# The last norm of a two-layer graph network: one-hot rows moved from ScalarE to VectorE, one row load of four moved from SyncE to ScalarE, Newton's steps once per seven batches

## The chip, the cores and the metric

The kernel runs on one core of one Trainium2 chip. The metric is the device time of one execution in microseconds, lower is better; a run's time is the median of several executions. The engines are named TensorE (PE in the profile; PEld is its weight load), VectorE (DVE), ScalarE (ACT), GpSimd (POOL) and SyncE (SP). A "q" behind a name (SPq, ACTq) is the instruction queue of that engine, from which DMAs are issued.

## The reference, cut to what matters

There are 100,000 nodes with 32 features and 25,000 edges. Two layers run one after the other, and each ends in a residual sum and a layer norm without learned weights:

```python
def _layernorm(x, axis=-1, eps=1e-05):
    m = jnp.mean(x, axis=axis, keepdims=True)
    v = jnp.var(x, axis=axis, keepdims=True)
    return (x - m) / jnp.sqrt(v + eps)
...
    x = _layernorm(x + _L0_gnn_ref(x, edge_weight1, edge_index, ...))
    x = _layernorm(x + _L1_gnn_ref(x, edge_weight, edge_attr_3, edge_index, ...))
```

The second layer makes a message per edge and adds it to the row of the edge's destination node (`out.at[dst].add(msg)`). The change is in what follows the messages: the adding into the nodes' rows, the second norm and the store of the result.

## The kernel before, in words

A window is 512 nodes, kept as 128 partitions of 4 nodes with 32 features, so 128 x 128 numbers; there are 196 windows (`NW`), all of them resident in on-chip memory in the tile `res`. A batch is G = 4 windows, so 128 x 512 numbers, and there are NB = 49 batches. The edges were sorted by destination window into 196 tiles of 128 rows in the DRAM tensor `placed[1]`, each row with 128 payload numbers and 8 more (`ROW` = 136 numbers, 544 bytes), the first of which says where the row belongs. Messages already have their mean taken away, so that the last norm needs only the sum of squares.

The last stage works through the 49 batches in a pipeline over five engines. Each engine has its instructions in an order written out by hand: `staged(stages, n)` (line 70) runs, in step s, the stages from the last to the first, stage k for batch s - k. Engines meet only through semaphores. For a batch b, before the change:

- SyncE (lines 498 to 500, helper `first_rows` at 374) waits until batch b - 6 has been multiplied, reads four tile numbers from memory into registers (line 376), and issues four loads (line 380), one for each window, into `pw4[b % 6]`, a ring of six. Each load is 68 KB.
- GpSimd (`apart_4`, 593) waits for the four loads and takes the difference between the window's first row and the place numbers: a 128 x 4 tile `kr4`, a ring of three. Before it, in the same step, stands `scale_4` (587) of ten batches earlier, which multiplies 128 x 512 numbers of `res` by 1/sqrt into `out4`, a ring of three.
- ScalarE (`away_from_4`, 804) takes |column - place| in four instructions of 128 columns into `away4`, then (`hot_4`, 811) max(0, 1 - that) in one of 512 columns: one-hot rows in `oh4`. Five steps after the first it squares the batch (`square_4`, 794), and eleven steps after it issues the store of the batch (`store_4`, 799), 256 KB.
- TensorE (1048 to 1053) multiplies the four one-hot tiles by the four payload tiles into a bank of PSUM.
- VectorE adds the bank to `res` (`add_4`, 1440) and three steps later sums the squares over 32 features (`norm_4`, 1445). Behind every fourth batch it runs `newton` (1338 to 1351): one addition, one shift-like step and three rounds of three instructions, eleven in all, each waiting for the one before, on 128 x 64 numbers (16 for each batch). The remainder, batch 48, gets eleven instructions of its own.

The waits that close the rings and that the prediction speaks of: a load waits for the multiplication five batches back (`z_mm`), `scale_4` waits for `z_root` of its group and for the store that left its buffer of `out4` (`z_st`).

## Time and profile before

| what | us |
|---|---|
| median of three runs (lowest, highest) | 1985.52 (1982.97, 1986.45) |
| span of the profiled execution, first to last instruction | 1707.1 |
| what lies around it, by the median less the span | 278.4 |
| the last stage in that span, from the first row load to the last instruction | about 151 |

The profile gives the profiled execution no total beside its span, so its own time is read as the span and the 278.4 us around it. In the page, busy time is the time in which an engine had an instruction in execution; instructions that read registers, wait for semaphores or issue DMAs are not counted, and are found in the timeline and in the chain of work under SPq, ACTq and DVEq. Durations overlap a little: the next instruction of an engine can start some 0.09 us before the end that is recorded for the one before.

### The profile page before, as it was taken

The page shows a single profiled execution, that of the slowest core. Times are in us where ns is not written, and L with a number is a line of the kernel's source. Part 1 is how long each engine was busy: PE and PEld are TensorE (multiplying, and loading weights), DVE is VectorE, ACT ScalarE, POOL GpSimd, SP SyncE. Part 2 cuts the span into 40 slices and gives each one's busy share as a digit, 9 for nine tenths or more (in the row PEclk, how much of TensorE's full clock was granted, in tenths as well). Part 3 has the DMA queues.
Part 4 walks back from the last instruction along what each step waited for, and adds up shares of the span by engine and source line. Part 5 has one row for each costly group of instructions (what it writes and reads, how often), then busy time and mean ns, then how long its engine had stood idle before and what let it go on. Part 6 is the DMA issues. An engine that isn't in the chain of part 4 may idle for free.

```text
span 1707.1 us, 25367 instructions
## 1 busy us (share of the span) xinstructions
PE 1315.9 (77%) x6200; PEld 957.6 (56%) x6200; DVE 1193.5 (70%) x3648; ACT 858.9 (50%) x2256; POOL 1068.9 (63%) x1168
## 2 busy tenths in 40 slices
PE   5699993686513777665778999958999999996673
PEld 1388881242212555554655666635777777775563
DVE  9699995677512443676667999964777777774776
ACT  0167770011101222666775777735666666664884
POOL 7777778777777777774111444448877887830444
PEclk8599996577555999888888999977999999997655
DMA  1000000123224988665555666531222222213785
GB/s 41 13 14 13 14 14 20 47 72 79 67 68 127 257 250 246 171 174 145 132 138 140 179 184 189 163 95 32 58 58 57 58 64 67 59 42 78 196 216 157
DMA packets 298498, 178.98 MB, mean 105 GB/s; under 512 B 28715, under 2 KB 290032, under 8 KB 298352
## 3 DMA queue, kind: packets, MB, share of 16 engines
q1 hardware_dynamic: 219712, 116.54, 26.0%
q0 software_dynamic: 29008, 36.18, 8.3%
q10 hardware_dynamic: 49632, 24.65, 5.0%
q8 instruction: 51, 0.84, 0.2%
q14 instruction: 95, 0.78, 0.2%
HBM read 111.18 MB, written 66.07 MB: 104 GB/s over the span
## 4 chain that ended last, share of the span: by engine, by line
PE 42%; POOL 28%; issue 16%; DVE 8%; DMA 2%; DVEq 2%; SPq 1%; ACT 1%; POOLq 0%; ACTq 0%
PE bank L1025 12%; POOL gat L511 12%; POOL lined L518 11%; PE bank L994 7%; PE bank L1018 7%; DVE res L1308 5%; PE bank L945 3%; POOL out L591 3%; PE bank L947 3%; PE bank L1034 3%; PE bank L1003 3%; PE bank L987 3%; DMA placed<-pay,pos_i 1%; DVEq L1308 1%; DVEq L1302 1%
## 5 line engine op out<-in xcount | busy, mean ns | idle before, releaser
L566 POOL DMA_INDIRECT gat<-x_d,src_i x196 | 253.2, 1292 | 59.0 <-issue 53.1
L511 POOL DMA_INDIRECT gat<-in_x,key_i x196 | 211.1, 1077 | 64.8 <-issue 62.4
L1308 DVE TENSOR_TENSOR res<-res,bank 128x128 f32 x588 | 168.4, 286 | 108.5 <-issue 24.4
L528 POOL DMA_INDIRECT placed<-pay,pos_i x196 | 191.9, 979 | 68.1 <-issue 65.6
L518 POOL DMA_INDIRECT lined<-in_x,other_i x196 | 195.8, 999 | 59.7 <-issue 59.7
L1025 PE MATMUL bank<-prod,ident 128*128 128x280 f32 x896 | 217.0, 400 | 0.0
L1025 PEld LDWEIGHTS bank<-prod,ident 128*128 128x128 f32 x896 | 171.0, 191 | 46.5 <-issue 0.6
L956 PE MATMUL bank<-woh,pw 128*128 128x128 f32 x784 | 135.4, 335 | 69.3 <-DVE woh L1287 33.4
L956 PEld LDWEIGHTS bank<-woh,pw 128*128 128x128 f32 x784 | 120.3, 238 | 85.5 <-DVE woh L1287 44.5
L56 ACT ACTIVATE xt<-bank 128x128 f32<-128x128 f32 x98 | 26.6, 271 | 269.6 <-PE bank L897 261.2
L1018 PE MATMUL bank<-rw,ht 65*128 65x384 f32 x392 | 141.3, 514 | 23.3 <-ACT ht L738 13.8
L553 POOL TENSOR_TENSOR hx<-hid,xin 128x512 f32<-128x512 f32 x49 | 62.0, 1264 | 136.2 <-ACT hid L724 136.2
L878 PE MATMUL bank<-tile_oh,sel 128*128 128x196 f32 x784 | 143.0, 337 | 3.1 <-ACT tile_oh L651 2.0
L878 PEld LDWEIGHTS bank<-tile_oh,sel 128*128 128x128 f32 x784 | 131.0, 193 | 17.3 <-issue 17.0
L1130 DVE SCALAR_TENSOR_TENSOR junk<-iota,w_f,bank 128x196 f32<-128x196 f32 x392 | 138.0, 408 | 0.9 <-PE bank L869 0.9
L994 PE MATMUL bank<-hid,wsl 128*128 128x512 f32 x294 | 134.9, 594 | 0.4 <-ACT hid L724 0.4
L56 ACT ACTIVATE rsb<-bank 128x384 f32<-128x384 f32 x196 | 95.5, 491 | 52.7 <-PE bank L1018 45.6
L1052 PE MATMUL bank<-pw,oh 128*128 128x128 f32 x392 | 89.6, 400 | 41.3 <-ACT oh L814 39.9
L689 ACT ACTIVATE woh<-iota,kr 128x128 f32<-128x128 f32 x294 | 93.8, 390 | 52.6 <-PE bank L956 26.0
L1018 PEld LDWEIGHTS bank<-rw,ht 65*128 65x128 f32 x392 | 75.8, 200 | 75.0 <-issue 17.9
L724 ACT ACTIVATE hid<-bank,bias 128x512 f32<-128x512 f32 x147 | 101.1, 688 | 31.2 <-PE bank L994 31.2
L1138 DVE TENSOR_TENSOR pay<-bank,wjs 128x512 f32<-128x512 f32 x49 | 33.8, 689 | 115.1 <-PE bank L902 115.0
(204 smaller groups left out, 2840.5 us busy)
## 6 DMA issues: line engine op xcount, KB each, us to landing
pw<-placed SPq DMA_DIRECT2D x588, 68.0 KB, 2.1
pw<-placed SPq DMA_DIRECT2D x98, 272.0 KB
xin<-in_x_t SPq DMA_DIRECT2D x53, 256.0 KB, 3.2
placed<-pay SPq DMA_DIRECT2D x49, 272.0 KB, 2.4
x_d<-res POOLq DMA_DIRECT2D x49, 256.0 KB, 3.8
placed<-pay SPq DMA_DIRECT2D x28, 448.0 KB, 3.2
out<-out ACTq DMA_DIRECT2D x49, 256.0 KB, 2.7
xin<-in_x_t ACTq DMA_DIRECT2D x45, 256.0 KB, 3.6
```

The lines of the kernel that those rows point to most:

```text
L56: return act.activation(out, in_, ACT.Copy)
L511: pool.indirect_dma_start(gat[:, t, :], None, x, bass.IndirectOffsetOnAxis(ap=key_i[:, 0, t:t + 1], axis=0)).then_inc(s_gat, 16)
L518: pool.indirect_dma_start(lined[i % LINED][:, k, :], None, x, bass.IndirectOffsetOnAxis(ap=other_i[:, t:t + 1], axis=0)).then_inc(s_lined[ ...
L528: pool.indirect_dma_start(placed[1].rearrange("t p r -> (t p) r"), bass.IndirectOffsetOnAxis(ap=pos_i[:, 1, t:t + 1], axis=0), pay[i % 4][ ...
L566: pool.indirect_dma_start(gat1[g % 3][:, k, :], None, x1_d, bass.IndirectOffsetOnAxis(ap=src_i[:, t:t + 1], axis=0)).then_inc(c_gat[g % 3] ...
L878: ins = pe.matmul(psum[4 + 2 * v][:, 0:NT], sel[g % 2][:, k, v, :], tile_oh[g % 2][:, k, :], start=t == 0, stop=t == NT - 1)
L956: ins = pe.matmul(quarter(bank, k), pw[i % 6][:, k, 0:P], woh[i % 4][:, k, :], start=True, stop=True)
L994: pe.matmul(psum[BANK[n][h]][:, :], wsl[:, 2 + n, :], hid[n - 1][h][:, :], start=True, stop=True).then_inc(m_mm[n], 1)
L1018: pe.matmul(psum[n % 3][:, 0:RC], ht[g % 2][:, P * k:P * k + P], rw[:, :, :].rearrange("p a b -> p (a b)"), start=True, stop=True).then_in ...
L1025: ins = pe.matmul(psum[3 + g % 2][:, 0:40 * U].rearrange("p (t u) -> p t u", t=U), ident[:, :], prod[g % 2][:, :, v, :], start=v == 0, sto ...
L1130: dve.scalar_tensor_tensor(out=junk[n % 4][:, :], in0=iota[:, :], scalar=w_f[:, c, t:t + 1], in1=column(n), op0=ALU.is_equal, op1=ALU.mult ...
L1308: add.up(dve.tensor_tensor(into, into, quarter(bank + k // G, k % G), ALU.add))
```

## The change: what it does, and the diff

One-hot rows. ScalarE's five instructions of a batch go, with the tile `away4` and the semaphore `z_away`. In their place VectorE compares, in one instruction of 512 columns, the column number with `kr4` (now place less window), both in on-chip memory. It stands last in VectorE's step, behind the square sum of four batches earlier and the addition of two batches earlier.

Row loads. SyncE reads three tile numbers and issues three loads; ScalarE reads the fourth number and issues the fourth load. It stands last in ScalarE's step, behind the store of 14 batches earlier and the square of 5 batches earlier. A new semaphore `z_stored` holds ScalarE's first load until SyncE has seen the stores of the stage before.

Newton's steps. They run once for seven batches, on 128 x 112 numbers, so seven times and not thirteen. `scale_4` moves from ten to thirteen batches behind `apart_4`.

```diff
+BY_SP = 3
+TOGETHER = 7
...
-        def first_rows(sp, to, c, b, landed):
+        def first_rows(eng, on, to, c, b, ks, landed):
             _, tiles = nc.values_load_multi_w_load_instructions(
-                t0_i[0:1, c, G * b:G * b + G], engines=[mybir.EngineType.SP], min_val=0, max_val=NT,
+                t0_i[0:1, c, G * b + ks.start:G * b + ks.stop], engines=[on], min_val=0, max_val=NT,
                 skip_runtime_bounds_check_because=IN_RANGE)
-            for k in range(G):
-                sp.dma_start(to[:, k, :], placed[c][bass.ds(tiles[k], 1)].rearrange("t p r -> p (t r)")).then_inc(landed, 16)
+            for k, tile in zip(ks, tiles):
+                eng.dma_start(to[:, k, :], placed[c][bass.ds(tile, 1)].rearrange("t p r -> p (t r)")).then_inc(landed, 16)
...
             sp.wait_ge(c_mm, NU)
+            sp.sem_inc(z_stored, 1)
             for b in range(NB):
                 wait(sp, z_mm, b - 5)
-                first_rows(sp, pw4[b % 6], 1, b, z_pw[b % 6])
+                first_rows(sp, mybir.EngineType.SP, pw4[b % 6], 1, b, range(BY_SP), z_pw[b % 6])
...
             def scale_4(b):
-                pool.wait_ge(z_root, b // 4 + 1)
+                pool.wait_ge(z_root, b // TOGETHER + 1)
...
             def apart_4(b):
                 pool.wait_ge(z_pw[b % 6], 16 * G * (b // 6 + 1))
-                wait(pool, z_away, b - 2)
-                pool.tensor_tensor(kr4[b % 3][:, :], w128[:, G * b:G * b + G], pw4[b % 6][:, :, P], ALU.subtract).then_inc(z_kr, 1)
-            staged([apart_4] + [None] * 9 + [scale_4], NB)
+                wait(pool, z_oh, b - 2)
+                pool.tensor_tensor(kr4[b % 3][:, :], pw4[b % 6][:, :, P], w128[:, G * b:G * b + G], ALU.subtract).then_inc(z_kr, 1)
+            staged([apart_4] + [None] * 12 + [scale_4], NB)
...
-            def away_from_4(b):
-                act.wait_ge(z_kr, b + 1)
-                wait(act, z_oh, b - 1)
-                for k in range(G):
-                    ins = act.activation(away4[b % 2][:, k, :], iota[:, 0:P], ACT.Abs, bias=kr4[b % 3][:, k:k + 1])
-                ins.then_inc(z_away, 1)
-            def hot_4(b):
-                act.wait_ge(z_away, b + 1)
-                wait(act, z_mm, b - 2)
-                act.activation(oh4[b % 3][:, :, :], away4[b % 2][:, :, :], ACT.Relu, bias=1.0, scale=-1.0).then_inc(z_oh, 1)
-            staged([away_from_4, hot_4, None, None, None, square_4] + [None] * 5 + [store_4], NB)
+            act.wait_ge(z_stored, 1)
+            def load_4(b):
+                wait(act, z_mm, b - 5)
+                first_rows(act, mybir.EngineType.Activation, pw4[b % 6], 1, b, range(BY_SP, G), z_pw[b % 6])
+            staged([load_4] + [None] * 4 + [square_4] + [None] * 8 + [store_4], NB)
...
             def norm_4(b):
-                four, o = b // 4, G * J * (b % 4)
+                n, o = b // TOGETHER, G * J * (b % TOGETHER)
                 dve.wait_ge(z_sq, b + 1)
...
-                if b % 4 == 3 or b == NB - 1:
+                if b % TOGETHER == TOGETHER - 1:
                     dve.wait_ge(z_ssq, b + 1)
-                    wait(dve, z_out, 4 * (four - 1))
-                    newton(vps4[:, 0:n], root4[four % 2][:, 0:n], newt4[:, 0:n], ssq4[four % 2][:, 0:n], z_root)
-            staged([add_4, None, None, norm_4], NB)
+                    wait(dve, z_out, TOGETHER * (n - 1))
+                    newton(vps4[:, :], root4[n % 2][:, :], newt4[:, :], ssq4[n % 2][:, :], z_root)
+            def hot_4(b):
+                dve.wait_ge(z_kr, b + 1)
+                wait(dve, z_mm, b - 2)
+                dve.tensor_tensor(oh4[b % 3][:, :, :], iota[:, 0:P].unsqueeze(1).broadcast_to([P, G, P]),
+                                  kr4[b % 3][:, :].unsqueeze(2).broadcast_to([P, G, P]), ALU.is_equal).then_inc(z_oh, 1)
+            staged([hot_4, None, add_4, None, norm_4], NB)
```

## Rows read from the trace of the kernel before

**Rows 1.** Span; windows: us, PE, PEld, DVE, ACT, POOL busy, PEclk, DMA, GB/s

```profile
span 1707.1 us, 25367 instructions
...
1553.00:1708.00 155.00, 92.34 (x405) 79.33 (x404) 100.59 (x248) 112.31 (x294) 59.51 (x98) 0.62 0.66 172
...
1620.00:1640.00 20.00, 14.69 (x64) 12.72 (x63) 15.80 (x38) 19.33 (x52) 10.09 (x17) 0.60 0.86 225
```

**Rows 2.** Waits in the last stage, in total, times, longest

```profile
POOL kr L596 <- DMA pw<-placed: 98.8, 42, 34.2
...
SPq L376 <- PE bank L1052: 1.1, 3, 0.6
```

**Rows 3.** Chain of work, SyncE's row loads: start us, us, what

```profile
1558.93 0.33 SPq L380
1559.45 0.33 SPq L380
...
1561.32 0.33 SPq L380
```

**Rows 4.** Timeline, GpSimd, first and last place difference: start us, us, what

```profile
1560.05 0.20 POOL L596 TENSOR_TENSOR kr<-w,pw 128x4 f32<-128x4 f32 x1 [34.20 <-DMA pw<-placed]
...
1681.94 0.20 POOL L596 TENSOR_TENSOR kr<-w,pw 128x4 f32<-128x4 f32 x1 [2.00 <-DMA pw<-placed]
```

**Rows 5.** Groups by line, last stage: busy us, mean ns, idle before

```profile
L808 ACT ACTIVATE away<-iota,kr 128x128 f32<-128x128 f32 x196 | 62.4, 389 | 28.5 <-POOL kr L596 27.9
L591 POOL TENSOR_TENSOR out<-res,root 128x512 f32<-128x512 f32 x49 | 51.2, 1049 | 15.1 <-DVE root L1348 11.3 <-ACT away L808 2.6 <-DMA out<-out 1.0
...
L814 ACT ACTIVATE oh<-away 128x512 f32<-128x512 f32 x49 | 30.1, 614 | 0.1
L797 ACT ACTIVATE sq<-res 128x512 f32<-128x512 f32 x49 | 30.1, 614 | 2.7 <-DVE ssq L1448 2.7
```

**Rows 6.** Timeline, one batch on GpSimd and VectorE

```profile
1626.35 0.20 POOL L596 TENSOR_TENSOR kr<-w,pw 128x4 f32<-128x4 f32 x1
1626.37 0.68 DVE L1443 TENSOR_TENSOR res<-res,bank 128x512 f32<-128x512 f32 x1
1626.50 1.05 POOL L591 TENSOR_TENSOR out<-res,root 128x512 f32<-128x512 f32 x1
...
1626.97 0.68 DVE L1448 TENSOR_REDUCE ssq<-sq 128x16 f32<-128x512 f32 x1
```

**Rows 7.** Timeline, VectorE around one run of Newton's steps, and its narrow form

```profile
1580.55 0.69 DVE L1448 TENSOR_REDUCE ssq<-sq 128x16 f32<-128x512 f32 x1 [2.49 <-ACT sq L797]
...
1583.80 0.23 DVE L1348 SCALAR_TENSOR_TENSOR root<-newt,root 128x64 f32<-128x64 f32 x1
1583.94 0.68 DVE L1443 TENSOR_TENSOR res<-res,bank 128x512 f32<-128x512 f32 x1
...
1698.02 0.17 DVE L1348 SCALAR_TENSOR_TENSOR root<-newt,root 128x16 f32<-128x16 f32 x1
```

**Rows 8.** Timeline, VectorE and GpSimd starting together

```profile
1633.36 0.29 POOL L596 TENSOR_TENSOR kr<-w,pw 128x4 f32<-128x4 f32 x1 [1.09 <-DMA pw<-placed]
1633.36 0.23 DVE L1344 TENSOR_TENSOR newt<-root 128x64 f32<-128x64 f32 x1
...
1682.10 1.05 POOL L591 TENSOR_TENSOR out<-res,root 128x512 f32<-128x512 f32 x1
1682.25 0.97 DVE L1344 TENSOR_TENSOR newt<-root 128x64 f32<-128x64 f32 x1
```

**Rows 9.** Chain of work: a register load on VectorE behind a compute instruction

```profile
1547.58 1.09 DVE pay L1420
1548.67 0.54 DVEq L1302
```

**Rows 10.** DMA issues, last stage: count, KB each, median us to landing

```profile
pw<-placed SPq DMA_DIRECT2D x196, 68.0 KB, 2.1
```

**Rows 11.** Timeline, one batch's multiplication at the lower clock

```profile
1583.29 2.08 PE L1052 MATMUL bank<-pw,oh 128*128 128x128 f32 x8 [1.05 <-ACT oh L814]
```

More of the change, by code:

```diff
@@ L38 @@
 IN_RANGE = "a prefix sum of counts that add up to the number of rows"
-assert NT == NW and NG * G == NT and NB == NG and 2 * HT == NT and NG % 7 == 0
+assert NT == NW and NG * G == NT and NB == NG and 2 * HT == NT and NG % 7 == 0 and NB % TOGETHER == 0
 assert PAD_NODE + NT * P - E <= NPAD <= OTHER and NPAD * P < 1 << 24
@@ L253, in gnn_kernel @@
         out4 = ring(sb, "out4", 3, [P, BC])
-        ssq4 = ring(sb, "ssq4", 2, [P, 4 * G * J])
-        root4 = ring(sb, "root4", 2, [P, 4 * G * J])
-        vps4 = sb("vps4", [P, 4 * G * J])
-        newt4 = sb("newt4", [P, 4 * G * J])
+        ssq4 = ring(sb, "ssq4", 2, [P, TOGETHER * G * J])
+        root4 = ring(sb, "root4", 2, [P, TOGETHER * G * J])
+        vps4 = sb("vps4", [P, TOGETHER * G * J])
+        newt4 = sb("newt4", [P, TOGETHER * G * J])
         psum = [ctx.enter_context(nc.psum_tensor(f"bank{n}", [P, 512], F32)) for n in range(8)]
@@ L291, in gnn_kernel @@
         c_prod, c_sum, c_scal, c_pay, c_mm, c_msg = sem("c_prod"), sem("c_sum"), sem("c_scal"), sem("c_pay"), sem("c_mm"), sem("c_msg")
[L293 removed]
+        z_pw, z_kr, z_oh, z_mm, z_stored = ring(sem, "z_pw", 6), sem("z_kr"), sem("z_oh"), sem("z_mm"), sem("z_stored")
         z_y, z_sq, z_ssq, z_root, z_out = sem("z_y"), sem("z_sq"), sem("z_ssq"), sem("z_root"), sem("z_out")
@@ L446, in _ @@
                 freed(sp, b - 5)
-                first_rows(sp, pw[b % 6], 0, b, s_pw[b % 6])
+                first_rows(sp, mybir.EngineType.SP, pw[b % 6], 0, b, range(G), s_pw[b % 6])
             def load_extra(i, c):
@@ L463, in _ @@
                 wait(sp, s_back, min(i - 5 - D_EXTRA, NG))
-                first_rows(sp, pw[i % 6], 1, b, s_pw[i % 6])
+                first_rows(sp, mybir.EngineType.SP, pw[i % 6], 1, b, range(G), s_pw[i % 6])
                 if b >= 5:
@@ L1445, in norm_4 @@
             def norm_4(b):
-                four, o = b // 4, G * J * (b % 4)
+                n, o = b // TOGETHER, G * J * (b % TOGETHER)
                 dve.wait_ge(z_sq, b + 1)
-                dve.tensor_reduce(ssq4[four % 2][:, o:o + G * J], nodes(sq4[b % 3][:, :]), AX_X, ALU.add).then_inc(z_ssq, 1)
-                if b % 4 == 3 or b == NB - 1:
-                    n = o + G * J
+                dve.tensor_reduce(ssq4[n % 2][:, o:o + G * J], nodes(sq4[b % 3][:, :]), AX_X, ALU.add).then_inc(z_ssq, 1)
+                if b % TOGETHER == TOGETHER - 1:
                     dve.wait_ge(z_ssq, b + 1)
-                    wait(dve, z_out, 4 * (four - 1))
-                    newton(vps4[:, 0:n], root4[four % 2][:, 0:n], newt4[:, 0:n], ssq4[four % 2][:, 0:n], z_root)
-            staged([add_4, None, None, norm_4], NB)
+                    wait(dve, z_out, TOGETHER * (n - 1))
[6 more added lines that the diff above has]
+            staged([hot_4, None, add_4, None, norm_4], NB)
 _INS = ["x", "src", "dst", "edge_attr_3", "edge_weight", "edge_weight1",
```

4 lines of the change are left out of this document (1 added, 3 removed).

## The prediction

> **What bounds the kernel now.** The change touches only the last stage, so I read the windows first. The stage takes the last 155 us of a span of 1707.1 us, and no engine fills it: ScalarE is busy 112 us, VectorE 101, GpSimd 60 [rows 1]. No engine being full, I looked for a queue. In the waits, GpSimd's place difference waits 98.8 us for row loads, 34.2 of it the one wait ahead of the stage, while SyncE waits for TensorE 1.1 us in all [rows 2]: the loads are late, and not because a buffer is missing. The chain of work shows why. SyncE issues a load every 0.52 us and starts the next batch's 2.39 us after the last batch's [rows 3]. That is its register read and four issues, one behind the other. The place differences are 121.9 us apart from first to last, 2.54 us a batch [rows 4], against 48 x 2.39 = 114.7 from issue alone; I put the other 7 us down to hiccups. So SyncE's issue sets the pace. Just under it lies ScalarE, busy 19.33 us of 20 in the middle of the stage [rows 1].
>
> **The base of the sum.** The profiled execution is its span, 1707.1, and what lies around it, which I take as 1985.5 - 1707.1 = 278.4 and leave alone. The sum is made on the span and set on the median.
>
> **The change, part by part.**
>
> *Three loads on SyncE.* Its pace becomes 2.39 - 0.52 = 1.87 us [rows 3]. That alone would be worth up to 0.52 x 48 = 25 us if nothing else stood near. TensorE stands near: a batch takes 2.08 us at the lower clock [rows 11], which the stage mostly has (granted 0.62 on average [rows 1]). With a hand-over I take 2.2 us as the pace that can be had before the other parts are looked at.
>
> *ScalarE.* It loses 4 x 0.389 + 0.614 us of work a batch [rows 5], on paper 2.2; I cost it as a gain only where ScalarE would have bound, which with three loads it would (19.33 of 20 us). It gets a register read and an issue. No register read of ScalarE is in the trace. On VectorE one was over 0.54 us after the compute instruction ahead of it had ended [rows 9]; on SyncE, with none ahead, read and register work come to about 0.3 of the 2.39 us. I take 0.54, because here too a compute instruction, the square, stands ahead. What is queued behind this new work matters more. In ScalarE's order the load of batch s stands behind the store of batch s - 14, the store behind GpSimd's scaling, the scaling behind the place difference of batch s - 2, and that behind its rows. This is a loop of two batches: from one place difference 0.15 us to the scaling's start [rows 6], 1.05 for it [rows 5], about 0.4 for the store's issue, 0.61 for the square [rows 5], 0.54 + 0.1 for the register read, 2.1 to the landing [rows 10]. The sum is 4.95, so 2.5 us a batch, and with landings 0.5 us later 2.75. Before batch 14 there is no store, and the loop is open.
>
> *VectorE's comparison.* Nothing of 512 columns with this operation is in the stage. Its neighbours of that size last 0.68 and start 0.60 apart [rows 6]; I take 0.60. VectorE then has three of these a batch, 1.79 us.
>
> *Newton's steps.* One run costs from the reduce before it to the addition behind it 3.39 - 0.60 = 2.79 us [rows 7]. Sixteen columns take 0.17 and 64 take 0.23 [rows 7], so 112 take 0.05 more: 2.79 + 11 x 0.05 = 3.34 us. Seven of these are 23.4 us; before they were 13, some 36. Per seven batches VectorE has 21 x 0.60 + 3.34 = 15.9 us, 2.27 a batch. By this count the change would gain.
>
> *What the count leaves out.* Both inputs of the comparison lie in on-chip memory, and beside it GpSimd scales. Rows 8 show such a pair: the scaling started at 1682.10 and ended at 1683.15; an instruction of Newton's, which takes 0.23 elsewhere, started at 1682.25 and ended at 1683.22. It stood until GpSimd was through. The other way round the cost is small there: the place difference took 0.29 rather than 0.20. The addition, with one input in PSUM, and the reduce, with one input, run at full speed inside a scaling [rows 6]. Before the change only Newton's steps could be caught, and GpSimd mostly waited for them. Now there is a comparison every batch, and the scaling starts 0.15 us behind the place difference that also releases a comparison. Each comparison can lose between 0 and 1.05 us. I take 0.5, the middle, because VectorE runs behind GpSimd and so meets the scaling at any phase. One scaling also falls into each run of Newton's steps: 1.05, between 0 and 2.1 for two. Per seven batches that is 12.5 + 3.34 + 1.05 + 3.5 = 20.4 us, 2.9 a batch, more than the loop's 2.5. VectorE becomes the bound, behind GpSimd.
>
> **The sum**, against 2.54 a batch. The first scaling comes 13 batches in; so long the pace is TensorE's: 13 x (2.2 - 2.54) = -4.4, and one run of Newton's steps that holds the additions back gives 1.4 again: -3. The remaining 35 batches: 5 x 20.4 - 35 x 2.54 = +13. The first one-hot rows come earlier, by ScalarE's 2.1 us less 0.7 and one issue of 0.52: -1.8. At the end seven scalings follow the last run of Newton's steps, where there was one group of four and a remainder: +1. Together +9, so 1985.5 + 9 = 1994.5 us.
>
> In the Trainium skill, "SBUF — State Buffer", section "Who interferes with whom", a VectorE instruction with two SBUF inputs contends with a GpSimd instruction that reads SBUF, and whichever starts first keeps the other out. The stalled instruction in the rows agrees; that a scaling waits behind a comparison of this length no row shows. By the rule each comparison also delays some scalings by up to its length; in the sum that would lengthen the loop, which has 0.4 us to spare, and leave the total about where it is.
>
> **The rivals.**
>
> *No collisions (faster).* VectorE and GpSimd settle so that the comparison falls between scalings, or a comparison with repeated inputs is not caught. Then the 35 batches go by the loop: 35 x (2.45 - 2.54) = -3, and the total is -3 - 3 - 1.8 + 1 = -7: 1978.5. For it: GpSimd needs only 1.25 us of the pace, so there is room. Against it: the scaling starts at the very event that releases a comparison, and Newton's instruction that began inside a scaling was held to its end [rows 8]. It decides where the stalls of seven batches, Newton's among them, come to under 2 us.
>
> *The loop alone.* Stalls are small, but the load on ScalarE lands late, 2.75 us a batch: 35 x 0.21 = +7.4, less 3.8 for the start and the end: 1989. For it: the row load stands directly behind a 256 KB store on the same queue, and the DMA engines are 0.86 busy already [rows 1]. Against it: nothing shows that landings grow.
>
> *Every comparison is caught in full.* 12.5 + 3.34 + 1.05 + 7.35 = 24.2 in seven batches, 5 x 24.2 - 88.9 = +32: 2014. For it: the common release. Against it: the norm and the addition stand in front of the comparison and use up 1.2 us, about a scaling's length.
>
> *It does nothing that can be measured.* A gain of SyncE's pace and the stalls cancel; no mechanism of its own, but the cases on either side meet here. A measurement of this kernel can tell about 0.2% from no change, 4 us.
>
> **How the numbers follow.** Forecast 0.50 (between 1990 and 2003 by stalls of 0.4 to 0.75); no collisions 0.22; the loop alone 0.18, a third of it within 4 us; full stalls 0.10. The forecast's lower end gives 0.08 to "same". So slower by over 0.2%: about 0.62; within it 0.16; faster 0.22. The range reaches from the case without collisions, 1979, up to 2006, half the way to the full stalls.
>
> **What would show each step right or wrong.** SyncE's issues should start to show waits for TensorE; if it still never waits, it is still the bound. The comparison's mean should be well over 0.68 us, with its ends on those of scalings, and 0.68 in the first 13 batches. Newton's runs should be seven, near 4.4 us. The place differences should be about 2.2 us apart at first and 2.9 later. On ScalarE, the load's issue should follow the square's end by 0.6 us. The forecast is wrong if the comparison's mean is near 0.68 or the later pace is below 2.6 us.

## The result, and the profile after

On the same chip, in 16 executions each, the kernel before took 1984.96 us (median; 1978.71 to 1990.50) and the changed kernel 1990.55 us (1986.35 to 1995.48). The ratio is 1.0026, with a 95% interval from 1.0013 to 1.0038. So the change makes the kernel slower by 0.26%, 5.6 us; the forecast was +9 us, with the time in the range.

**A correction first.** The profiled execution of the changed kernel took 1989.1 us, and its span is 1987.3: only 1.8 us lie around a span. The 278 us that I put "around the span" of 1707.1 do not. To see what they are, I profiled the kernel before once more, unchanged:

> The kernel before, once more with a profile. The span of its first profile was 1707.1 us where its runs take 1985; the changed kernel's profile has a span of 1987.3 and a time of 1989.1. If what lies outside the span was a property of the kernel, this profile has a span near 1707 again; if it was a property of that one execution, the span is near 1983 and the last stage again takes about 150.6 us from its first row load to the last instruction, which is the only part the comparison rests on.

It took 1994.16 us with a span of 1992.4, so the 1707.1 and the 1985.5 were different executions of the same program. Later runs confirm it: on one chip the kernel before has a median of 1709.09 us (29 executions), on another 1706.82, on two more 1992.07 and 1985.64. The page's row of bytes moved, in 40 slices of the span, shows where the difference lies. The first is the profile of [rows 1]:

```profile
GB/s 41 13 14 13 14 14 20 47 72 79 67 68 127 257 250 246 171 174 145 132 138 140 179 184 189 163 95 32 58 58 57 58 64 67 59 42 78 196 216 157
```

The second is the same kernel in the execution of 1992.4 us:

```profile
GB/s 37 13 13 12 14 4 1 1 1 39 40 51 68 63 74 159 203 196 189 119 145 122 135 132 166 184 183 169 83 42 51 65 64 51 65 65 38 154 219 163
```

Slices 6 to 9 of the second move almost nothing (1 to 4 GB/s), and the rise to 150 and more comes at slice 16 rather than 14. All of it is in the early stages, which the change does not touch: the first row load of the last stage comes at 1556.5 us in the one and at 1843.3 in the other. What makes the early stages longer on some chips was not looked into. The last stage, from the first row load to the last instruction, lasts 150.6 us in the one and 149.1 in the other. So stages can be compared across chips, and whole times only with the kernel before on the same chip. I do that throughout. A stage is read from one profile of each kernel, and the two profiles of the kernel before are 1.5 us apart, so a difference of that size between two stages says nothing. Every kernel below computes the whole output.

**The last stage of the changed kernel** lasts 157.0 us, 6.4 to 7.9 more than before. In windows of it (columns as in [rows 1]), its start, the steady part with scaling, and its end:

```profile
1829.00:1862.00 33.00, 18.25 (x88) 16.01 (x88) 23.84 (x48) 5.67 (x9) 3.69 (x14) 0.76 0.47 117
1862.00:1953.00 91.00, 50.20 (x275) 44.47 (x273) 84.36 (x152) 21.42 (x34) 44.43 (x68) 0.74 0.77 203
1953.00:1988.00 35.00, 8.02 (x32) 7.13 (x32) 17.29 (x33) 3.78 (x6) 16.61 (x17) 0.50 0.44 124
```

VectorE is busy 84.4 of 91 us, where before it had 101 of 155 and ScalarE 112 [rows 1]. ScalarE has 21.4 of 91 left. The groups by line of the whole stage, answering to [rows 5]:

```profile
L593 POOL TENSOR_TENSOR out<-res,root 128x512 f32<-128x512 f32 x49 | 53.3, 1093 | 7.4 <-DVE root L1344 6.2 <-DMA out<-out 1.0
L1453 DVE TENSOR_TENSOR oh<-iota,kr 128x512 f32<-128x512 f32 x49 | 41.3, 843 | 5.8 <-POOL kr L598 5.6
L1444 DVE TENSOR_REDUCE ssq<-sq 128x16 f32<-128x512 f32 x49 | 33.2, 677 | 4.8 <-ACT sq L799 4.6
...
L799 ACT ACTIVATE sq<-res 128x512 f32<-128x512 f32 x49 | 30.9, 630 | 117.1 <-DVE res L1439 69.0 <-POOL out L593 25.5 <-PE bank L1048 19.5
L598 POOL TENSOR_TENSOR kr<-pw,w 128x4 f32<-128x4 f32 x49 | 13.1, 268 | 108.2 <-DMA pw<-placed 107.3 <-DVE oh L1453 0.8
```

Three things are to be seen. The comparison lasts 843 ns on average. The scaling went from 1049 [rows 5] to 1093, and the place difference from some 200 [rows 4] to 268. And the place difference still waits for row loads, 107.3 us, as it did before [rows 2].

**The collisions.** Timeline of VectorE and GpSimd at two places, some 4 us apart:

```profile
1906.15 0.68 DVE L1453 TENSOR_TENSOR oh<-iota,kr 128x512 f32<-128x512 f32 x1
1906.21 1.53 POOL L593 TENSOR_TENSOR out<-res,root 128x512 f32<-128x512 f32 x1
...
1910.54 1.05 POOL L593 TENSOR_TENSOR out<-res,root 128x512 f32<-128x512 f32 x1
1910.62 1.51 DVE L1453 TENSOR_TENSOR oh<-iota,kr 128x512 f32<-128x512 f32 x1 [0.20 <-POOL kr L598]
```

In the first pair the comparison began 0.06 us earlier and ran at full speed, and the scaling took 1.53 us instead of 1.05. In the second the scaling began first and ran at full speed, and the comparison took 1.51 instead of 0.68. Whichever starts first keeps the other out, as far as the starts can be told apart: one comparison is recorded 0.02 us after a scaling (1925.91 and 1925.89) and still took 0.68, and the scaling took 1.60. This is the rule that the prediction drew from the Trainium skill ("SBUF — State Buffer", section "Who interferes with whom"), and the trace agrees with both directions of it. Of the 49 comparisons 15 took over 0.9 us, each beside a scaling that had begun before it; none of the first eleven did, as no scaling runs yet. Of the scalings 7 took over 1.1 us: four beside a comparison (1.49 to 1.60), three beside a short instruction of Newton's steps (1.13 to 1.17).

**The loop through ScalarE's queue.** The same stretch, now with ScalarE's issues and the place differences; it is the loop that the prediction wrote out:

```profile
1904.60 0.49 POOL L598 TENSOR_TENSOR kr<-pw,w 128x4 f32<-128x4 f32 x1 [2.09 <-DMA pw<-placed]
1905.05 1.05 POOL L593 TENSOR_TENSOR out<-res,root 128x512 f32<-128x512 f32 x1
1906.06 0.19 POOL L598 TENSOR_TENSOR kr<-pw,w 128x4 f32<-128x4 f32 x1
1906.13 0.46 ACTq L803 DMA_DIRECT2D out<-out  x1
...
1906.69 0.63 ACT L799 ACTIVATE sq<-res 128x512 f32<-128x512 f32 x1 [3.01 <-PE bank L1048]
...
1907.43 0.34 ACTq L381 DMA_DIRECT2D pw<-placed  x1
...
1910.40 0.20 POOL L598 TENSOR_TENSOR kr<-pw,w 128x4 f32<-128x4 f32 x1 [2.65 <-DMA pw<-placed]
```

Place difference, scaling, store, square, load and, 2.97 us after its issue, the place difference two batches on: 5.8 us for two batches. In 31 of the last 35 batches ScalarE's load was issued later than SyncE's last one for the same batch (on average 2.7 us against 4.8 before the place difference).

VectorE has a hand in this loop too, because the square waits for VectorE's addition of the same batch. Two batches earlier than the stretch above:

```profile
1899.29 0.45 ACTq L803 DMA_DIRECT2D out<-out  x1
...
1900.18 0.67 DVE L1439 TENSOR_TENSOR res<-res,bank 128x512 f32<-128x512 f32 x1
...
1900.89 0.63 ACT L799 ACTIVATE sq<-res 128x512 f32<-128x512 f32 x1 [1.80 <-DVE res L1439]
1901.40 0.37 ACTq L381 DMA_DIRECT2D pw<-placed  x1
```

Here the store's issue ends at 1899.74, and the square, with the load behind it, starts 1.15 us later, 0.03 after the addition. In 26 of the last 35 batches the square starts 0.10 us after the store's issue ends. In the other 9, two behind each of four runs of Newton's steps and one behind a fifth, it starts 0.03 us after the addition, 0.9 to 2.1 us later than the store alone would have let it.

**SyncE.** The chain of work, its register read and loads of the second batch:

```profile
1831.82 0.67 SPq L377
1832.53 0.04 SPq L381
1832.66 0.33 SPq L381
...
1833.18 0.33 SPq L381
```

and in the kernel before the read of four numbers:

```profile
1558.47 0.30 SPq L376
```

The read of three numbers takes 0.66 to 0.68 us (28 of 49 times; 0.82 on average), the read of four took 0.30. The pace of SyncE came out as 2.2 to 2.3 us and not as 1.87.

### The profile page after: what moved, and what is told of

The parts are those of the page before. It is cut to its first block, busy times and chain, and to the rows that moved or that the text cites. A ratio compares the mean times of both kernels' runs of the same rounds, so it can differ in the third digit from the quotient of the medians.

```text
span 1987.3 us, 25104 instructions
## 1 busy us (share of the span) xinstructions
PE 1345.6 (68%) x6200; PEld 968.7 (49%) x6200; DVE 1224.3 (62%) x3631; ACT 775.2 (39%) x2011; POOL 1060.1 (53%) x1168
## 3 DMA queue, kind: packets, MB, share of 16 engines
q1 hardware_dynamic: 212656, 113.13, 21.4%
## 4 chain that ended last, share of the span: by engine, by line
PE 39%; DVE 26%; issue 19%; another core or an unknown queue 10%; DVEq 2%; POOL 1%; DMA 1%; SPq 1%; ACT 1%; ACTq 0%; POOLq 0%
PE bank L1021 11%; PE bank L990 6%; PE bank L1014 6%; DVE junk L1126 5%; DVE res L1304 5%; DVE oh L1096 4%; DVE sel L1198 4%; PE bank L941 3%; PE bank L943 2%; PE bank L1030 2%; PE bank L983 2%; PE bank L999 2%; PE bank L874 1%; DVEq L1304 1%
## 5 line engine op out<-in xcount | busy, mean ns | idle before, releaser
L530 POOL DMA_INDIRECT placed<-pay,pos_i x196 | 191.9, 979 | 136.0 <-issue 126.1
L513 POOL DMA_INDIRECT gat<-in_x,key_i x196 | 196.0, 1000 | 64.6 <-issue 62.4
L864 PE MATMUL bank<-oh,lower 128*128 128x392 bf16 x196 | 80.0, 408 | 170.1 <-DVE junk L1126 105.2
L1126 DVE SCALAR_TENSOR_TENSOR junk<-iota,w_f,bank 128x196 f32<-128x196 f32 x392 | 142.6, 436 | 73.1 <-remote 46.2
L874 PE MATMUL bank<-tile_oh,sel 128*128 128x196 f32 x784 | 154.5, 351 | 27.6 <-issue 25.2
L874 PEld LDWEIGHTS bank<-tile_oh,sel 128*128 128x128 f32 x784 | 139.3, 202 | 45.1 <-issue 44.7
L58 ACT ACTIVATE pos_i<-pos_f 128x4 int32<-128x4 f32 x98 | 20.1, 205 | 345.8 <-DVE junk L1126 268.9
L58 ACT ACTIVATE xt<-bank 128x128 f32<-128x128 f32 x98 | 26.5, 271 | 311.7 <-PE bank L893 163.4
L1198 DVE TENSOR_SCALAR sel<-iota,rt_f,val 128x128 f32<-128x128 f32 x196 | 76.1, 388 | 104.1 <-remote 76.7
L1134 DVE TENSOR_TENSOR pay<-bank,wj 128x512 f32<-128x512 f32 x49 | 33.8, 690 | 155.4 <-remote 74.0
L864 PEld LDWEIGHTS bank<-oh,lower 128*128 128x128 bf16 x196 | 21.2, 108 | 213.9 <-issue 161.1
L1048 PE MATMUL bank<-pw,oh 128*128 128x128 f32 x392 | 76.3, 362 | 60.4 <-DVE oh L1453 60.0
```

The costliest lines, as they stand in the source:

```text
L513: pool.indirect_dma_start(gat[:, t, :], None, x, bass.IndirectOffsetOnAxis(ap=key_i[:, 0, t:t + 1], axis=0)).then_inc(s_gat, 16)
L530: pool.indirect_dma_start(placed[1].rearrange("t p r -> (t p) r"), bass.IndirectOffsetOnAxis(ap=pos_i[:, 1, t:t + 1], axis=0), pay[i % 4][ ...
L874: ins = pe.matmul(psum[4 + 2 * v][:, 0:NT], sel[g % 2][:, k, v, :], tile_oh[g % 2][:, k, :], start=t == 0, stop=t == NT - 1)
L1126: dve.scalar_tensor_tensor(out=junk[n % 4][:, :], in0=iota[:, :], scalar=w_f[:, c, t:t + 1], in1=column(n), op0=ALU.is_equal, op1=ALU.mult ...
L1198: ins = dve.tensor_scalar(sel[g % 2][:, k, v, :], iota[:, 0:P], rt_f[g % 3][:, 0, k:k + 1], values[:, t:t + 1], ALU.is_equal, ALU.mult)
```

## The experiments

Times of the last stage below run from SyncE's first row load: to the last place difference, and to the last instruction. "Pace" is the mean distance of the place differences over batches 0 to 13, and 13 to 48. The tail is what follows the last of them. The ratios come from four chips, on which the kernel before takes 1992.07 us (e1 to e3), 1709.09 (e4 to e7), 1985.64 (e8 to e10) and 1706.82 (e11).

| kernel | last place difference | end | pace early, late | tail | ratio to before (95%) |
|---|---|---|---|---|---|
| before, two profiles | 125.5, 123.5 | 150.6, 149.1 | 2.57, 2.53; 2.51, 2.50 | 25.1, 25.6 | 1 |
| changed | 127.7 | 157.0 | 2.25, 2.71 | 29.3 | 1.0026 (1.0013 to 1.0038) |
| e1 loads alone | 122.2 | 148.1 | 2.38, 2.52 | 25.9 | 0.9991 (0.9976 to 1.0005) |
| e2 column numbers in PSUM | 126.4 | 153.1 | 2.35, 2.64 | 26.8 | 1.0016 (1.0004 to 1.0029) |
| e3 four loads on SyncE | 125.4 | 154.5 | 2.53, 2.55 | 29.1 | 1.0029 (1.0016 to 1.0042) |
| e4 loads alone, read of four | 112.7 | 140.0 | 2.02, 2.37 | 27.3 | 0.9951 (0.9929 to 0.9972) |
| e5 changed, read of four | 123.5 | 152.2 | 1.97, 2.70 | 28.7 | 1.0013 (0.9984 to 1.0042) |
| e6 Newton alone | 126.1 | 152.6 | 2.54, 2.56 | 26.5 | 1.0013 (0.9992 to 1.0034) |
| e7 rows shared by batch | 145.9 | 174.2 | 2.22, 3.25 | 28.3 | 1.0127 (1.0096 to 1.0158) |
| e8 rows alone | 129.8 | 159.8 | 2.56, 2.66 | 30.0 | 1.0044 (1.0028 to 1.0060) |
| e9 e2 and e5 together | 121.7 | 148.3 | 2.01, 2.63 | 26.6 | 0.9988 (0.9974 to 1.0001) |
| e10 one window of four | 124.2 | 152.3 | 1.99, 2.71 | 28.1 | 1.0014 (1.0001 to 1.0027) |
| e11 e4, scaling a step later | 111.4 | 139.3 | 1.96, 2.36 | 27.9 | 0.9932 (0.9910 to 0.9953) |

**The loads alone (e1).** The kernel before, with only the fourth load on ScalarE. Its place in ScalarE's order is four steps ahead of the one-hot rows, so that it does not stand behind a store it depends on.

```diff
+BY_SP = 3
...
-            staged([away_from_4, hot_4, None, None, None, square_4] + [None] * 5 + [store_4], NB)
+            staged([load_4, None, None, None, away_from_4, hot_4, None, None, None, square_4] + [None] * 5 + [store_4], NB)
```

> Only the row loads are changed against the kernel before: three on SyncE, one on ScalarE, there four steps ahead of the one-hot rows it serves; one-hot rows stay on ScalarE, Newton's steps run per four batches. Theory A (the split of the loads is the part that gains, and the move of the one-hot rows to VectorE gives the gain back): SyncE's 2.39 us a batch falls to 1.87, ScalarE's 2.2 us becomes the bound, the place differences come 2.25 to 2.35 us apart and the stage is 9 to 13 us shorter than 150.6: about 1974 us, ratio 0.994. Theory B (ScalarE cannot take an issue without losing as much: it is busy 19.3 of 20 us): pace 2.5 or more, ratio 0.999 to 1.004.

Measured: 0.9991, no difference that can be told, and a late pace of 2.52. Theory A missed. The ratio is Theory B's, and the pace nearly so, but not for its reason: SyncE waited for TensorE 1.2 us in all, issued one load fewer and was hardly faster, because its register read was long again (0.67 early, 0.85 on average later). What that read costs was a new question. e4 answers it, and shows that ScalarE can take the issue.

**Reading four numbers and using three (e4).**

```diff
-                t0_i[0:1, c, G * b + ks.start:G * b + ks.stop], engines=[on], min_val=0, max_val=NT,
+                t0_i[0:1, c, G * b + ks.start:G * b + (G if ks.start == 0 else ks.stop)], engines=[on], min_val=0, max_val=NT,
```

> As the kernel with the loads alone changed (its stage took 148.1 us), but SyncE reads four tile numbers from memory at once and uses three. In the kernels with a split, a read of three numbers took 0.67 us and more on SyncE, a read of four 0.30 in the kernel before, so SyncE's pace with three loads is 2.2 to 2.5 and not 1.87. Theory A (the read of three numbers eats the issue that was saved): reads are back at 0.3, SyncE's pace is 1.9 until it waits for free buffers, place differences come about 2.3 us apart, the stage takes 138 to 143 us, ratio 0.993 to 0.996. Theory B (reads are long because both queues read at the same time; ScalarE and TensorE bind anyway): reads stay over 0.5 us or the pace stays at 2.45, ratio 0.998 or more.

Measured: 0.9951, the stage 140.0 us, 8.1 less than e1, as Theory A said. The edit changes how many numbers are read, and nothing else. e1 and e4 ran on different chips, but their ratios to the kernel before differ in the same way and their intervals do not meet. The waits of its stage:

```profile
POOL kr L599 <- DMA pw<-placed: 46.4, 8, 34.3
...
POOL out L594 <- DVE root L1357: 37.2, 13, 4.1
...
POOL out L594 <- DMA out<-out: 13.9, 18, 1.6
```

After the first wait of 34.3 us only 12.1 us of waiting for loads are left, where there were 64.6 [rows 2]. In none of the last 35 batches was ScalarE's load the later one. What is full now is ScalarE: over these batches it is busy 96% of the time, 2.27 of 2.37 us a batch. So the split of the loads is worth 9 to 11 us of stage if the read is short and the load on ScalarE stands where nothing that depends on it stands ahead of it.

**The same read in the changed kernel (e5).** The edit of e4, made in the changed kernel.

> The changed kernel with that same read of four. Theory A (VectorE binds from the second run of Newton's steps on): only the first 13 batches gain, 0 to 2 us, ratio 1.001 to 1.003. Rival (SyncE's slow read was what held the changed kernel): the stage falls from 157.0 to 150 us or less, ratio at most 0.999.

Measured: a stage of 152.2 us, 4.7 less. That is more than Theory A's 0 to 2 and not the 7 of the rival, and nearly all of it lies where Theory A had it, in the first 13 batches (pace 1.97 instead of 2.25). Later it is 2.70, as in the changed kernel, and ScalarE's load is the last one in 35 of 35 batches. SyncE's pace does not matter once the loop through ScalarE is closed: it now waits for TensorE 18.6 us, mostly in four waits of 3.7 to 4.2 us, once in seven batches. (A load waits until the batch six before it has been multiplied, as its buffer is one of six.) The ratio, 1.0013, has an interval too wide to tell it from either kernel.

**Column numbers from PSUM (e2).** The changed kernel; 128 columns are copied once into a free bank, and the comparison has only one input in on-chip SBUF.

```diff
+            chain.up(dve.tensor_copy(psum[7][:, 0:P], iota[:, 0:P]))
+            done(chain)
...
-                dve.tensor_tensor(oh4[b % 3][:, :, :], iota[:, 0:P].unsqueeze(1).broadcast_to([P, G, P]),
+                dve.tensor_tensor(oh4[b % 3][:, :, :], psum[7][:, 0:P].unsqueeze(1).broadcast_to([P, G, P]),
```

> The changed kernel, but the column numbers of the comparison are read from a free bank of PSUM, so that only one of its inputs lies in on-chip SBUF memory. Theory A (comparison and scaling keep each other out because both read SBUF with two inputs): the comparison's mean falls from 0.843 to about 0.69 us, no scaling is over 1.06 us, place differences are back at 0.20; the stage falls from 157.0 to 148 to 152 us, ratio to the kernel before 0.996 to 1.000. Theory C (VectorE is simply full with three instructions of 512 columns and Newton's steps; the collisions fall into time that is lost anyway): the stage stays at 155 us or more, ratio 1.002 or more.

The groups by line of its stage:

```profile
L593 POOL TENSOR_TENSOR out<-res,root 128x512 f32<-128x512 f32 x49 | 51.2, 1050 | 6.8 <-DVE root L1344 5.3 <-DMA out<-out 1.6
L1456 DVE TENSOR_TENSOR oh<-bank,kr 128x512 f32<-128x512 f32 x49 | 33.6, 686 | 7.0 <-POOL kr L598 6.9
...
L598 POOL TENSOR_TENSOR kr<-pw,w 128x4 f32<-128x4 f32 x49 | 10.0, 204 | 110.1 <-DMA pw<-placed 109.9
```

All three are back at their undisturbed durations: 686 ns for 843, 1050 for 1093, 204 for 268. The comparison's collisions are gone, and VectorE has 7.7 us less to do in comparisons. Newton's steps, whose inputs are not in PSUM, are still held: one run takes up to 4.86 us, and 3.25 where no scaling runs. The stage is only 3.8 us shorter, 153.1, and the late pace is 2.64; this lies between the two theories. By the stage, the comparison's collisions are about half of the 6.4 to 7.9 us that were lost. The whole times can't say it: the intervals of this kernel and the changed one overlap. What is left in the late pace is the loop: ScalarE's load is the later one in 29 of 35 batches, and 9 of its squares wait for VectorE's addition, as before.

**All four loads on SyncE (e3).** The changed kernel with `BY_SP = 4` and no `load_4` in ScalarE's order.

```diff
-BY_SP = 3
+BY_SP = 4
...
-            staged([load_4] + [None] * 4 + [square_4] + [None] * 8 + [store_4], NB)
+            staged([None] * 5 + [square_4] + [None] * 8 + [store_4], NB)
```

> The changed kernel, but SyncE issues all four row loads again and ScalarE none. Theory A (VectorE bounds the later batches at about 2.6 us, SyncE's 2.39 us would be hidden there): only the first 13 batches get slower, by 13 x 0.2 = 3 us; ratio about 1.003 to 1.006. Rival (the load on ScalarE, behind store and square, is late and holds the place differences): without it the stage gets shorter or stays, ratio at most 1.002.

Measured: 1.0029, the same as the changed kernel and just below Theory A's range; that the stage gets shorter (154.5 us) is what the rival said. Within the stage two things moved against each other: the early pace went from 2.25 to 2.53, SyncE's issue again, and the late pace from 2.71 to 2.55. The loop through ScalarE was worth 0.16 us a batch, which is more than the loss at the start. The waits of its later batches (1863 to 1960 us), and SyncE's of the whole stage:

```profile
POOL kr L598 <- DMA pw<-placed: 46.8, 32, 2.7
...
POOL kr L598 <- DVE oh L1453: 3.5, 5, 0.7
```

```profile
SPq L377 <- PE bank L1048: 0.9, 3, 0.5
```

SyncE hardly ever waits for a buffer, and the place differences wait for landings and not for VectorE. So in e3 it is again SyncE's issue that sets the pace (2.53 early, 2.55 late), and not VectorE, as Theory A had it. VectorE, busy 95% of these batches, just keeps up.

**Newton's steps alone (e6).** The kernel before, in groups of seven, with the scaling 13 batches behind and the store three steps later.

```diff
+TOGETHER = 7
...
-            staged([apart_4] + [None] * 9 + [scale_4], NB)
+            staged([apart_4] + [None] * 12 + [scale_4], NB)
```

> The kernel before with Newton's steps once for seven batches, scaling 13 and store 14 steps behind, and nothing else. SyncE sets the pace and VectorE has room, so work saved on VectorE gains nothing before the last batch: last place difference 122 to 124 us after the first load, as before. Theory A (the end gets longer, since seven scalings, each about 1.2 us with the ring of three stores, follow the last run): 1 to 3 us more behind it, ratio 1.0005 to 1.002. Rival (one run at the end instead of two makes the end shorter): ratio 0.999 or less.

Measured: 1.0013, not told apart from no change; the pace is that of before (2.54, 2.56), and the tail is 26.5 against 25.1 and 25.6, 0.9 to 1.4 us longer. VectorE saves work that the kernel before had no use for.

**The one-hot rows alone (e8).** The kernel before with the comparison on VectorE; four loads on SyncE, groups of four.

```diff
-            staged([add_4, None, None, norm_4], NB)
...
+            staged([hot_4, None, add_4, None, norm_4], NB)
```

> The kernel before with the one-hot rows made by VectorE in one comparison, and nothing else: four loads on SyncE, Newton's steps per four batches. Theory A (moving the rows to VectorE is what costs, and the grouping by seven pays part of it back): VectorE has 7 x 1.79 + 7/4 x 3 us and the collisions, 18.5 to 20 us in seven batches, 2.65 to 2.8 each; the stage takes 156 to 162 us, ratio 1.003 to 1.006. Rival (the rows on VectorE are free, the change loses by its other parts): stage 148 to 152, ratio at most 1.001.

Measured: 1.0044 and a stage of 159.8 us, the longest of the three parts taken alone, and as Theory A said. The comparison:

```profile
L1446 DVE TENSOR_TENSOR oh<-iota,kr 128x512 f32<-128x512 f32 x49 | 42.6, 869 | 6.9 <-POOL kr L596 6.9
```

So this is the part that costs. Here VectorE is full: between batches 13 and 48 it is busy 97% of the time, and place differences wait for its comparisons in 21 places. Against e3, which is this kernel with Newton's steps in groups of seven, it is 5.3 us longer. On a VectorE that is full, the larger groups seem to pay; but e3 also scales 13 and not 10 batches behind, and GpSimd's wait for Newton's result is 8.6 us there and 29.1 here, so how much is the work saved and how much the distance was not separated.

**Both mends (e9).** The changed kernel with the edits of e2 and e5.

> The changed kernel with SyncE reading four numbers and with the column numbers in PSUM. Each alone took the stage from 157.0 to 152.2 and 153.1 us. Theory A (one gains in the first batches, the other in the later ones, and they add): 147 to 150 us, ratio 0.997 to 1.000. Rival (VectorE is full either way, they overlap): 151 to 153, ratio 1.001 or more.

Measured: 148.3 us, 8.7 less than the changed kernel; the two gains, 3.8 and 4.7, add, as Theory A said. The whole times agree, as the intervals of this kernel and the changed one do not meet. With both, the change is about level with the kernel before (0.9988, the interval holds 1), and still 8 us of stage behind e4.

**Every other batch (e7).** VectorE makes the rows of even batches from PSUM columns, ScalarE those of odd ones, the rest as e5. Its `hot_4` on VectorE returns on odd batches, and ScalarE's order becomes:

```diff
-            staged([load_4] + [None] * 4 + [square_4] + [None] * 8 + [store_4], NB)
+            staged([load_4, None, None, None, away_from_4, hot_4, None, None, None, square_4] + [None] * 8 + [store_4], NB)
```

> One-hot rows of even batches on VectorE in one comparison (column numbers in PSUM), of odd batches on ScalarE in its five instructions; loads split with the read of four, Newton's steps once for seven batches. By the counts VectorE needs 12.5 - 7 x 0.3 + 4.1 us in seven batches, 2.1 each; ScalarE 1.4; SyncE 1.87; TensorE 2.2 at the lower clock. Theory A (the engines' work, spread evenly, is the limit): place differences 2.2 to 2.35 us apart, stage 137 to 143 us, ratio 0.992 to 0.996. Rival (the DMA engines, 0.86 busy at 2.4 us a batch, or the landings bind before that): pace 2.4 or more, ratio 0.998 or more.

Measured: 1.0127 and a stage of 174.2 us. Theory A missed by far. The rival's bounds were open at the top and hold, but nothing points to its cause: the DMA engines are busy 57% of the stage. The waits of its stage:

```profile
PE bank L1071 <- DVE oh L1481: 71.0, 23, 7.1
...
POOL out L599 <- DMA out<-out: 49.7, 30, 4.8
DVE ssq L1470 <- ACT sq L808: 49.4, 24, 3.2
```

No engine is full (VectorE 99.7 and ScalarE 70.8 of 176 us); everybody waits for somebody. My reading is that two hand-written orders which each alternate between a long and a short step hand their delays to each other. That was only read from the waits, not tested.

**One window of four (e10).** e4, with VectorE making the rows of the first window (128 columns) straight from the landed rows.

```diff
-                for k in range(G):
+                for k in range(1, G):
...
-            staged([add_4, None, None, norm_4], NB)
+            staged([first_4, None, add_4, None, None, norm_4], NB)
```

> As the loads alone with the read of four (stage 140.0 us), but VectorE makes the one-hot rows of the first window of each batch, 128 columns, and ScalarE those of three. ScalarE's 2.2 us a batch become 1.8, VectorE gets 0.3 more on 1.9. Theory A (ScalarE is the bound of that kernel): the place differences come 2.2 us apart rather than 2.28 and the stage takes 134 to 138 us, ratio 0.992 to 0.994. Rival (TensorE at the lower clock, or the waits between the engines, bind at the same pace): stage 139 us or more, ratio 0.995 or more.

Measured: 1.0014, the stage 152.3 us, 12 more than e4. Theory A missed, and the rival, whose bounds hold, expected about the same pace and not a worse one. Its waits:

```profile
POOL out L594 <- DVE root L1358: 31.6, 12, 4.2
POOL out L594 <- DMA out<-out: 31.1, 18, 3.9
```

GpSimd waits no longer for Newton's result than in e4 (37.2 us there), so that is not the difference. The trace shows another one. The multiplication now needs rows from VectorE, and these stand in VectorE's order behind Newton's steps. In 19 of the last 35 batches, at least two behind each run of Newton's steps, the first window's rows were ready after ScalarE's three, 30 us later in all, and the multiplication began 0.1 to 0.2 us after them. SyncE's waits for TensorE grew from 6.0 to 19.3 us. The instruction itself is a small part (395 ns on average, where 280 is undisturbed). That this is what costs the 12 us is read from the trace; no run moved these rows ahead of Newton's steps.

**The scaling a step later (e11).** e4, with one step more between place difference and scaling, and the store after it.

```diff
-            staged([apart_4] + [None] * 9 + [scale_4], NB)
+            staged([apart_4] + [None] * 10 + [scale_4], NB)
```

> e4_loads_read_four with GpSimd's scaling eleven batches behind the place difference and not ten, and the store one step later to match. In e4_loads_read_four GpSimd waited 37.2 us in 13 places for Newton's result, about 2.9 us each, and the place differences came in fours, 4.2 and then 1.2, 1.6 and 2.5 us apart. Theory A: that wait is on the path, because the next place differences stand behind the waiting scaling; one step more gives the result one batch of time. The wait falls below 15 us, the pitch evens out, the last place difference comes 2 to 6 us earlier than 112.7 us behind the first load, and with one scaling more at the end (1.05 us) the stage lasts 136 to 139.5 us; against the kernel before, 7 to 11 us less, a ratio of 0.9935 to 0.997. Theory B: ScalarE, busy 111.7 of 140 us there, or TensorE sets the average and the waves are only its shape; the wait shrinks but the stage lasts 139.5 to 142 us. Either way it also shows whether the split with a read of four is faster on another chip, should the chip be one: A and B both expect a ratio of at most 0.998.

Its waits:

```profile
POOL out L594 <- DMA out<-out: 24.8, 19, 2.2
...
POOL out L594 <- DVE root L1357: 13.9, 9, 2.7
POOL out L594 <- ACT away L817: 10.0, 10, 1.8
```

The wait for Newton's result fell from 37.2 to 13.9 us as both theories said, but waits for the store and for ScalarE took most of its place. The last place difference comes 1.3 us earlier, less than Theory A's 2 to 6, and the stage ends at 139.3 us, inside Theory A's range by 0.2 us. So the wait was mostly the shape of a limit that lies elsewhere: ScalarE, with 111.6 us of work, is again busy 96% of the last 35 batches. The ratio is 0.9932 (1693.33 us against 1706.82). This and e4 beat both kernels; whether e11 beats e4 their intervals can't say. Both ran on chips on which the kernel before takes about 1708 us. The gain was not measured on a slower chip, where the same 8 to 13.5 us would be 0.4 to 0.7%.

## Why the prediction was right, and where its steps were not

**Direction and size.** Forecast +9 us by VectorE becoming the bound in the later batches; measured +5.6. That the time came out in the range is in part luck: the later batches were priced 6.5 us too high and the end 4.9 too low. By the last place difference and the tail, against the first profile of the kernel before, the sum reads: first 13 batches -3 (measured -4.3), 35 later ones +13 (measured +6.5), the tail +1 less the 1.8 of the first rows, so -0.8 (measured +4.1). Right were the direction, the collisions as a cause (e2) and that moving the rows is what costs (e8). Not right was the mechanism of the later pace: VectorE was not the bound of the place differences, the loop through ScalarE was.

**First rows.** Forecast 1.8 us earlier (the terms given add up to 1.9). From the first load, they start at 3.67 us and not at 5.17: 1.5. Nearly right, but the last of the terms was not there: the first place difference came 0.13 us earlier and not one issue (0.52).

**First 13 batches.** The forecast pace of 2.2 was met (2.25), but for another reason. The step that failed is "its pace becomes 2.39 - 0.52 = 1.87": it took the register read along as unchanged. With three numbers it costs some 0.4 us more and gave most of the saved issue back. TensorE, which I had made the limit, was not: of SyncE's waits for it, 8.7 us in 14 places, only 1.0 us falls before 1863 us, and in e5 the early pace is 1.97. In the changed kernel half of the saving was lost there without being seen; e5 has it back.

**The comparison's stall.** The step "I take 0.5, the middle" was mis-sized. It was 0.19 us on average over the last 35 batches (13 of them were caught, by 0.51 us each) and 0 over the first eleven. The mechanism and its sign were right, and e2 removes the stalls by taking away one of the shared inputs. The middle between 0 and 1.05 was not the row-based choice that it looked like. A comparison stalls only where it starts inside a scaling, and then for what is left of it; the scalings take 1.05 of 2.7 us, which gives (1.05 / 2.7) x 0.52 = 0.20 for a start at any phase. That could have been worked out beforehand from [rows 5] and the forecast pace. It is an estimate and no better than that: in e3, e5 and e8, where the same sum also gives about 0.2, the mean stall is 0.17, 0.27 and 0.25.

**Newton's runs.** Seven, as said, of 3.25, 4.11, 4.86, 3.98, 4.56, 4.03 and 3.26 us. The first, before any scaling runs, is the forecast 3.34 without collisions. The forecast's 4.4 is for a run beside scalings, and the five between the first and the last have a mean of 4.3: right.

**VectorE as the bound.** Per seven of the later batches VectorE's work comes to 21 x 0.60 + 7 x 0.19 + 4.3 = 18.2 us, 2.6 a batch, and not 20.4. The step "VectorE becomes the bound" failed with it. In e3 VectorE has the same work and ScalarE issues no load; the late pace is 2.55, and there it is SyncE's issue and not VectorE that the place differences wait for. So VectorE's work alone does not make 2.71. The loop through ScalarE does: in 31 of the 35 batches its load is the last. I had it as a rival of its own, "the loop alone", priced at 2.75 a batch, and let the larger of the two win. They work together. The waits for VectorE's addition that were shown above are 10.9 us in 35 rounds of a loop of two batches, which is 0.16 us a batch of the 2.71. The failed step is to treat the two limits as alternatives, with the pace that of the larger. A loop of five engines that also contains a busy one takes delays from both.

**Within the loop** two terms were wrong and one was missing. "I take 0.54, because here too a compute instruction stands ahead": ScalarE's read of one number takes 0.28 to 0.30 us (45 of 49 times) and starts 0.01 to 0.03 us after the square, not behind it. The issue comes some 0.47 us after the square's start. Against it, landing took longer than the 2.1 us: 2.4 in the median, 2.7 on average until the place difference begins. Missing was the wait of the square for the addition, 0.31 on average. The sum, 4.95 for two batches, came out as 5.4 on average (2 x 2.71) and 5.8 in the stretch shown.

**The end.** The step "seven scalings follow the last run: +1" left out that VectorE runs behind. Its last comparison starts 4.2 us after the last place difference and ends after 5.7; in the kernel before ScalarE's last rows were ready 2.6 us after it. Then come the sum of squares, Newton's steps and the seven scalings, which wait for the stores that leave their buffers. The chain of work of the changed kernel at the end:

```profile
1971.37 1.06 POOL out L593
1972.42 0.02 issue
1972.45 2.35 DMA out<-out
```

e6 has Newton's groups without a late VectorE, and its tail is 0.9 to 1.4 longer than before: the forecast +1 was right for this part alone. The last run of Newton's steps ends 10.5 us after the last place difference in e6 and 13.3 in the changed kernel; from there to the end both take 16.0 to 16.1 us. So 2.7 of the 4.1 us are the lateness, and the rest is the grouping.

**The base.** "What lies around it" is 1.8 us and not 278. It did no harm to the sum, as the last stage is about equally long on both kinds of chip (150.6 and 149.1).

**The rivals.** No collisions (1978.5): fell, 15 of 49 comparisons were caught. Full stalls: fell. The loop alone (1989): its mechanism is there with nearly its pace (2.71 for 2.75), and the time, 1990.55, is nearer to it than to the forecast. What it lacked were the stalls and the end. Nothing measurable: fell, as the interval begins at 1.0013.

## What to carry to other kernels

Before work is moved from a full engine to a half-full one, ask whether the full one is the bound: here the queue that issued loads was, and the one part of the change that went to it was worth 8 us and more when done well, while moving the rows cost as much. Put an issue into an engine's order where nothing ahead of it depends, through other engines, on what it loads; otherwise it closes a loop that no faster neighbour opens. For two engines that shut each other out, take as a first estimate of the stall the share of time in which the other one runs, times half its length, and try whether one input can be read from PSUM.

## What the runs showed of the hardware

- A register read on SyncE of three numbers took 0.66 us at best, one of four 0.29, and one of a single number on ScalarE 0.28. With reads of four on one queue and of one on the other (e4) SyncE's took 0.44 on average and the first 0.47; e1 and e4, on different chips, differ only in this and by 8.1 us of stage. Why three is slower than four no run shows.
- A register read and a DMA issue on ScalarE's queue do not wait for the ACTIVATE ahead of them: one issue began at 1903.52, 0.47 us after the start (1903.05) of a square that lasts 0.63.
- A place difference of 128 x 4 numbers, 0.20 us long, took 0.64 when it began 0.09 us after a comparison: the shut-out holds small instructions too.
- With one input in PSUM instead of SBUF the comparison of 512 columns took 686 ns on average and 0.69 us at most, scalings running beside it, and the scalings 1050.
- The same program takes about 1708 us on some chips and 1985 to 1992 on others, with all of the difference in its early stages.
